# A decoder layer on one core: query rows sent as diagonal blocks, self attention over pairs of batches, preparation and second layer norm drawn into the self loop, one product for the maxima

## The reference, cut to what matters

```python
# x: 16 batches x 56 tokens x 128; ctx: 16 x 1500 x 128; bias: 16 x 1500; 16 heads of 8
x = x + self_attention(layernorm(x))                  # qkv with bias, scores / sqrt(8), softmax, projection
x = x + cross_attention(layernorm(x), ctx, bias)      # bias added to the scores before the softmax
x = x + experts(layernorm(x))                         # top 4 of 32 experts, and one shared expert
```

## Time and profile before

| what | value |
|---|---|
| median of 3 runs | 533.33 us (532.56 to 533.93) |
| the profiled execution, its own time | 532.37 us |
| its span in the trace | 530.6 us |
| PE busy, share of the span | 455.5 us, 86% |
| DVE | 377.0 us, 71% |
| ACT | 345.5 us, 65% |
| POOL | 261.1 us, 49% |
| mean granted clock of PE | 0.93 of full speed |

### The profile page before, as it was taken

One profiled execution on the slowest core, in us unless ns is written; L12 is line 12 of the kernel. 1 busy time (PEld: TensorE's weight loads), 2 busy tenths in 40 slices (PEclk: granted clock), 3 DMA queues, 4 the chain that ended last, 5 costly groups with the idle time before them and its releaser, 6 DMA issues.

```text
span 530.6 us, 16284 instructions
## 1 busy us (share of the span) xinstructions
PE 455.5 (86%) x6841; PEld 297.1 (56%) x6841; DVE 377.0 (71%) x603; ACT 345.5 (65%) x716; POOL 261.1 (49%) x207
## 2 busy tenths in 40 slices
PE   3225898568999999999999999999989886799995
PEld 2013676234677677667677667667766653344442
DVE  6752445878777777777777777777778234899994
ACT  6802654424788788788788888888876772355552
POOL 4399005458668568558657756751400310145430
PEclk9757889865999999999999999999999997899998
DMA  6991069183768674794694695483202020011101
GB/s 129 226 260 56 3 129 209 53 236 110 128 205 204 124 165 143 123 194 124 114 208 125 125 186 107 115 94 97 89 12 61 13 51 1 16 45 46 30 1 35
DMA packets 79758, 58.24 MB, mean 110 GB/s; under 512 B 62350, under 2 KB 69830, under 8 KB 79686
## 3 DMA queue, kind: packets, MB, share of 16 engines
q1 hardware_dynamic: 78886, 57.15, 48.3%
q0 software_dynamic: 512, 0.03, 0.1%
q10 hardware_dynamic: 288, 0.03, 0.0%
HBM read 17.01 MB, written 0.46 MB: 33 GB/s over the span
## 4 chain that ended last, share of the span: by engine, by line
PE 61%; DVE 12%; issue 10%; ACT 5%; POOL 2%; DVEq 0%; POOLq 0%; ACTq 0%
PE ps L925 18%; PE ps L814 12%; PE ps L903 6%; DVE mx L1514 3%; PE ps L817 3%; DVE v L1609 3%; ACT v L1269 3%; PE ps L368 3%; PE ps L370 3%; PE ps L369 3%; PE ps L824 2%; PE ps L744 2%; PE ps L747 2%; PE ps L745 2%; PE ps L962 1%
## 5 line engine op out<-in xcount | busy, mean ns | idle before, releaser
L1514 DVE TENSOR_REDUCE mx<-ps 120x2 f32<-120x1000 f32 x192 | 221.1, 1195 | 66.8 <-PE ps L903 66.7
L1209 ACT ACTIVATE p<-ps 125x448 f32<-125x448 f32 x288 | 140.6, 543 | 9.0 <-PE ps L925 7.5
L925 PE MATMUL ps<-qall,ks 128*125 128x224 f16 x768 | 134.4, 278 | 6.0 <-ACT p L1209 2.8
L925 PEld LDWEIGHTS ps<-qall,ks 128*125 128x125 f16 x768 | 75.7, 137 | 46.4 <-ACT p L1209 23.1
L620 POOL TENSOR_TENSOR k<-k,zero 128x500 f16<-128x500 f32 x45 | 45.9, 1021 | 92.8 <-ACT k L1145 92.8
L814 PE MATMUL ps<-p,v 125*27 125x168 f32 x1280 | 72.8, 312 | 0.0
L600 POOL TENSOR_TENSOR ch<-ctx,zero 128x1536 f16<-128x1536 f32 x16 | 44.0, 2748 | 41.5 <-issue 27.8
L624 POOL TENSOR_TENSOR k<-k 128x500 f16<-128x500 f32 x45 | 51.1, 1135 | 3.5
L610 POOL TENSOR_TENSOR ch<-ctx,ch 128x1536 f16<-128x1536 f32 x16 | 51.4, 3212 | 1.3
L1209 ACT ACTIVATE wnat<-ps 125x448 f32<-125x448 f32 x96 | 47.0, 541 | 7.5 <-PE ps L925 7.5
L903 PE MATMUL ps<-ks,qall 31*56 31x500 f16 x768 | 44.8, 407 | 6.7 <-DVE mx L1514 6.6
(11 more groups left out here) (178 smaller groups left out, 811.6 us busy)
## 6 DMA issues: line engine op xcount, KB each, us to landing
ks<-k SPq DMA_DIRECT2D x48, 375.0 KB
ctx<-in_ctx SPq DMA_DIRECT2D x16, 672.0 KB
ks<-in_L_ffn_W SPq DMA_DIRECT2D x48, 64.0 KB, 2.0
qall<-late SPq DMA_DIRECT2D x6, 448.0 KB, 6.9
ks<-brow SPq DMA_DIRECT2D x32, 46.9 KB
qall<-qd SPq DMA_DIRECT2D x3, 448.0 KB, 8.5
ctx<-in_ctx SPq DMA_DIRECT2D x16, 78.0 KB
qall<-qconst SPq DMA_DIRECT2D x1, 896.0 KB, 10.3
```

Source lines behind the costliest of these rows:

```text
L925: last = mm(stb[half][0:KP, 224 * (g % 2):224 * (g % 2) + 224], ks[c % 3][:, g, KP * s:KP * s + KP], qall[:, g, 3 * r + c].rearrange("p h ...
L1209: A(p[s % 4][0:KP, 448 * half:448 * half + 448], stb[half][0:KP, 0:448], ACT.Exp, scale=SCALE).then_inc(exp_done, 1)
L1514: V.tensor_reduce(mx[:, h:h + 2, k // 2], mxb[0:120, 2 * pair:2 * pair + 2, 0:CH], axis=AX.X, op=ALU.max).then_inc(mx_read, 1)
```

## The change

`qall` changes its order from group, batch, head to group, head, batch. POOL fills it with zeros once, and the queries of 32 partitions go straight from `q1` and `q2` into the rows of their own head: four transfers a row for all batches of self attention, and the same for cross attention, now in the parts of two and of fourteen batches. The mask, `qd`, `first_queries` and `second_queries` go. Self attention runs over pairs of batches, the second at partitions 64 to 119 (11 steps instead of 19). Batch 0 and the keys of batch 1 are prepared inside these steps. LN2 is split into one tile and six. The maxima of the cross loop take one product of 16 columns. The two selects of `pairsel` move on POOL behind the last key split. The diff, cut to its core (what stands behind a # names the engine or the place):

```diff
-PARTS = [((0, B // 2), (B // 2, B)), ((0, 4), (4, B // 2), (B // 2, B))]
-EARLY = 1
-OUT_STEP = 13
+PAIRS = B // 2
+PARTS = ((0, 2), (2, B))
+PREP = {1: (0, "K0"), 2: (0, "K1"), 3: (0, "K2"), 4: (0, "V0"), 5: (0, "V1"), 6: (0, "V2"),
+        7: (1, "K0"), 8: (1, "K1"), 9: (1, "K2")}
+OUT_STEP, TURN_STEP, Q_STEP = 5, 7, 8
...
-        qall = sb("qall", [128, G, B, HG, S], F16)
+        qall = sb("qall", [128, G, HG, B, S], F16)
+        LN_TILES = (TILES, ((0, 1), (1, TT)), TILES)
+        QX = ((0, S * PARTS[0][1]), (S * PARTS[0][1], T))
+        def query_rows(engine, n, k, row, part, done):
+            a, z = ((0, B),)[k] if n == 0 else PARTS[k]
+            src = (q1, q2)[part]
+            for j in range(HG):
+                engine.dma_start(qall[32 * j + row:32 * j + 32:4, :, j, a:z].rearrange("p g b q -> p g (b q)"),
+                                 src[32 * j:32 * j + 32, S * a:S * z]).then_inc(done, 16)
...
             load_ctx(0)
+            sp.wait_ge(qconst_ok, 1)
+            sp.wait_ge(qzero_ok, 2)
+            for j in range(HG):
+                sp.dma_start(qall[32 * j + HI_ROW:32 * j + LO_ROW + 1:4, :, j].rearrange("p g b q -> p g (b q)"),
+                             qconst[0:2].rearrange("p (o x) -> p o x", o=1).to_broadcast([2, G, T])).then_inc(qfill_ok, 16)
+            sp.wait_ge(q1_ok, 2)
+            for row in range(2):
+                query_rows(sp, 0, 0, row, 0, qs_ok[0])
             load_ctx(1)
...
             bias_rows(0)
             bias_rows(1)
-            key_stacks(0)
             transpose_ctx(1)
             load_ctx(3)
+            key_stacks(0)
+            sp.wait_ge(st_done, 1)
+            sp.wait_ge(q1_ok, 3)
+            for row in range(2):
+                query_rows(sp, 1, 0, row, 0, qx_ok[0][0])
             transpose_ctx(2)
             load_ctx(4)
             key_stacks(1)
+            sp.wait_ge(st_done, PAIRS)
+            sp.wait_ge(q1_ok, 4)
+            for row in range(2):
+                query_rows(sp, 1, 1, row, 0, qx_ok[1][0])
+            sp.wait_ge(q2_ok, 4)
+            query_rows(sp, 1, 1, 2, 1, qx_ok[1][1])
             transpose_ctx(3)
             load_ctx(5)
...
+            def zero_queries(n):                                     # POOL
+                memset(qall[:, 2 * n:2 * n + 2].rearrange("p g h b q -> p (g h b q)").bitcast(F32), 0.0
+                       ).then_inc(qzero_ok, 1)
...
+            zero_queries(0)
             rstd_of(0, 0)
             rstd_of(0, 1)
+            zero_queries(1)
...
+            rstd_of(1, 0)
             split_first(2)
             split_second(2)
-            rstd_of(1, 0)
-            rstd_of(1, 1)
             for j in range(3):
                 split_keys(1, j)
+            rstd_of(1, 1)
             split_first(3)
             split_second(3)
...
+            def self_max_rows(half):                                 # PE
+                pe.wait_ge(mself_ok, 4 * half + 4)
+                for upper in range(2):
+                    rows = slice(64 * upper, 64 * upper + S)
+                    for b in range(8):
+                        last = mm(ps[0:8, (4, 2)[half] + upper, S * b:S * b + S],
+                                  mself[rows, half, :, :, b].rearrange("p g j -> p (g j)"),
+                                  ident[rows, rows], start=True, stop=True)
+                last.then_inc(mselft_psum, 1)
...
+            def self_step(s):                                        # PE
+                k = s % 2
+                if s < PAIRS:
+                    pe.wait_ge(mself_row[s // 4], 2 * 16)
...
+                    for g in range(G):
+                        for u in range(2):
+                            b = 2 * s + u
+                            last = mm(sbank[64 * u:64 * u + S, g // 2, 224 * (g % 2):224 * (g % 2) + 224],
+                                      kself[:, g, S * b:S * b + S], qall[:, g, :, b], start=True, stop=True)
+                    last.then_inc(st_done, 1)
+                    if s == 0:
+                        self_max_rows(1)
...
+                if 0 <= s - 3 < PAIRS:
+                    tr(pair_misc[:, 0:128], tok[:], ident[:]).then_inc(misc_done, 1)
+                if s in PREP:
+                    b, use = PREP[s]
+                    prepare[use[0]](0, b, int(use[1]))
+                if 0 <= s - 1 < PAIRS:
+                    pair_times_v(1 - k)          # 16 products, the two batches at rows 0 and 64, banks 6 and 7
+                if 0 <= s - 2 < PAIRS:
+                    pick_pair()
...
                 elif use == "mt":
                     pe.wait_ge(mcol_ok, 3 * r + c + 2)
-                    for j in range(HG):
-                        last = mm(misc[0:G, S * j:S * j + S], mcol[:, j::HG], fold[:], start=True, stop=True)
-                    last.then_inc(misc_done, 1)
+                    mm(misc[0:H, 0:S], mcol[:], fold[:], start=True, stop=True).then_inc(misc_done, 1)
...
                         last = mm(stb[half][0:KP, 224 * (g % 2):224 * (g % 2) + 224],
                                   ks[c % 3][:, g, KP * s:KP * s + KP],
-                                  qall[:, g, 3 * r + c].rearrange("p h q -> p (h q)"),
-                                  start=True, stop=True)
+                                  qall[:, g, :, 3 * r + c], start=True, stop=True)
...
+            query_rows(act, 0, 0, 2, 1, qs_ok[1])                    # ACT, before the self loop
+            for row, part in ((0, 0), (1, 1), (2, 0)):
+                act.dma_start(ks[2][row::4, :, 0:T], k12[:, part, 0:T]).then_inc(kself_in, 16)
...
+                elif j == 0:
+                    act.wait_ge(brow_ok, 1)                          # ACT, key part K0 of batch 0
+                A(k32[:, cols], use_bank(r, c, f"K{j}")[:, 0:CH], ACT.Copy).then_inc(use_read(r, c, f"K{j}")[0], 1)
...
+                if s == Q_STEP:                                      # ACT
+                    A(q1[:, a:z], chain_bank[:, 0:z - a], ACT.Copy).then_inc(q1_ok, 1)
+                    act.wait_ge(q2_ok, 3)
+                    query_rows(act, 1, 0, 2, 1, qx_ok[0][1])
...
             add_to_x(LN_TILES[1][1], flat_bank(0, 768), x_ok)        # DVE
             norm_stats(1, 1)
-            norm_apply(1, 1)
...
+            take_round(0, -2, 2, 0)
+            norm_apply(1, 1)
+            for k in range(1, ROUNDS // 2):
                 take_round(0, -2, 2, k)
```

More of the change, by code:

```diff
@@ L117, in part_of, with prep_index, self_uses, self_index @@
 def part_of(b):
-    return [a <= b < z for a, z in PARTS[1]].index(True)
-def early(r, c):
-    return isinstance(r, int) and 3 * r + c < EARLY
+    return [a <= b < z for a, z in PARTS].index(True)
+def prep_index(b, use):
+    return PREP_ORDER.index((b, use)) if (b, use) in PREP_ORDER else None
 def round_of(d):
     return (1, d + 3) if d < 3 else (2, d - 3)
[L132 to L147, removed]
+def self_uses(s):
+    return [u for u, lag in (("tr", 3), ("sel", 2)) if 0 <= s - lag < PAIRS]
+def self_index(s, use):
+    return sum(len(self_uses(k)) for k in range(s)) + self_uses(s).index(use)
 def build(nc, x_d, ctx_d, bias_d, qkv_w, qkv_b, proj_w, proj_b, wq, wk, wv, wo,
@@ L298, in build @@
         mselfr_ok = sem("mselfr_ok")
-        mself_row = sem("mself_row")
+        mself_row = [sem(f"mself_row{n}") for n in range(2)]
         st_done = sem("st_done")
@@ L687, in split_experts @@
                                         ).then_inc(wh_ok, 1)
+            for n, row0 in enumerate((0, 32)):
+                pool.wait_ge(pairsel_step, n + 1)
+                select(out=pairsel[:], in_=pairsel[:], compare_op=ALU.not_equal, fill=1.0, base=-row0,
+                       pattern=[[-2, NP], [-1, 2], [0, HE]], channel_multiplier=1).then_inc(pairsel_step, 1)
             rstd_of(2, 0)
@@ L712, in transpose_norm @@
             def transpose_norm(n, half, bank, done):
[L714 to L717 removed]
+                a, z = LN_TILES[n][half]
+                pe.wait_ge(xn_ok, TT * n + z)
+                out = flat_bank(bank, 128 * (z - a)) if z - a > 4 else ps[:, bank]
+                for j in range(a, z):
+                    last = tr(out[:, 128 * (j - a):128 * (j - a) + 128], xn[:, j], ident[:])
                 last.then_inc(done, 1)
@@ L772, in _ @@
                 project(SELF_W, half, 4 + half, q_psum)
+            for half in range(2):
                 project(SELF_W + 1, half, 6 + half, k_psum)
@@ L877, in router_logits @@
+            pe.wait_ge(pick_ok, 1)
+            for s in range(PAIRS + 3):
+                self_step(s)
             def router_logits(half, bank):
@@ L1203, in exponential @@
+            self_max_rows(0)
+            for s in range(PAIRS + 3):
+                self_step(s)
+            norm_out(1, 1, 0, xt_psum, 3)
+            act.wait_ge(pv_done, PAIRS)
             def exponential(r, c, s, half):
-                tile = B + KT * (3 * r + c) + s
+                tile = PAIRS + KT * (3 * r + c) + s
```

(7 more changed lines are left out.)

577 lines of the change are left out of this document (253 added, 324 removed).

## The result

The changed kernel takes 517.91 us, the median of 4 runs (517.17 to 518.73), where the kernel before took 532.98 beside it (532.56 to 533.93). The ratio is 0.9715, with a 95% interval of 0.9693 to 0.9737: 15.1 us faster. The prediction was 508.2 with a range of 499 to 519, and a gain of 25. The direction and the range held; ten of the 25 us did not come.

What follows compares the result with a forecast made beforehand. PE bounds the cross loop; before it, waits and single steps do. First cross scores 19.6 us earlier, plus 1.0 for masks and 4.5 for products, give 25.1: from 533.33 to 508.2 us, range 499 to 519.

Steps and rivals of the forecast that it cites:

- Loop period: Cross loop, bound by PE: three of four products mt go, 0.28 us in each of 15 iterations, 4.5 us with the copy.
- strided queries: Cross loop: score products reading four runs of 56 elements cost zero extra; the opposing slower case had chance 0.04.
- single maximum product: Cross loop: one product mt in place of four saves 3 x 0.09 = 0.28 us per iteration.
- first cross scores: Milestone before the cross loop: from 128.83 to 109.2, about 17.6 us after the query projection.
- removed masks: Cross loop: the last masks, 2.33 us of ACT in the chain, go; partly covered, worth 1.0 us.
- Selects: Before self attention: PE's 4.46 us wait for pairsel goes; moving the selects on POOL costs nothing.
- First maximum round: First milestone, in self attention: from 30.68 to 27.5, bounds 25 and 31, summed from projections, copies, issues and landing.
- First self scores: Second milestone: from 52.84 to 41.0, with 3.4 us for the block of 16 small products.
- Self loop: Third milestone, the loop's end: from 95.89 to 74.5, at 3.0 us per step of a pair of batches.
- bias operation: Self step 0: 2.81 us on DVE delays ACT's first key part; step 3 starts near 50.3 instead of 48.5.
- Behind the loop: Loop's end to cross query projection: 17.1 us, reaching 91.6 instead of 111.47; six normalization tiles cost 4.
- The first one: Pairs do not run side by side, or the path behind the loop grows: 517.5 with steps alone, 523 with all; chance 0.20.

Runs made afterwards that it cites:

- second profile of the changed kernel: The changed kernel, unedited, run once more beside its variants as the base for small differences: 518.75 us.
- that run: The kernel before with only the two pairsel selects moved late on POOL, PE's wait put ahead of the experts: 527.95 us against 534.77.
- the kernel of four products: The changed kernel with the four products mt per batch, their copy and transfer put back in the cross loop: 520.66 us.

## Why the prediction was right, and where ten microseconds went

- **Loop period, strided queries, single maximum product: right.** 5.5 us were predicted behind the first cross scores, 5.7 came, and 4.6 in the second profile of the changed kernel (517.3 - 120.11 = 397.2); the score products cost what they did; the single product gives 4.4 us by the periods. The 1.0 us for the removed masks wasn't tested, and the clock differs in that stretch.
- **Selects: right.** "I see no use of theirs before the experts: nothing" holds, and the wait they caused was worth 4 to 4.5 us by the profile of that run.
- **First maximum round: wrong by 4.8 us.** Two steps failed. "POOL's new zero fill [...] hidden behind the projections" priced only POOL's own time; it held LN1 on DVE for 3.8 us, and the run without that gave 2.9 back at the end. "SP's context loads [...] are passed by four fills and eight query issues" priced only when the context is wanted. What it missed is that the load of batch 1 moves beside the keys: the landing, taken as 5 us, was 6.9 to 7.2 with it and 2.8 without. I had measured the old crowd and removed it without asking which transfer comes in its place. In the terms of the sum: the projections ended at 32.30 - 12.40 = 19.9 and not at 16.4, and the landing took 1.9 more. The seven issues on ACT took 5.8 us and not 4.2, but they ran beside the key copies, so that the last one ended 5.4 us behind the projections where 5.8 were costed.
- **First self scores: 2.2 us better.** The block was costed at 3.4 us and took 2.75, and the four other rounds with the copy and the hand-over took 43.58 - 39.65 = 3.9 us (the end of the block is at 39.7) where 5.3 were costed.
- **Self loop: short by 3.7 us.** Part of it is a slip of the sum. From step 1 at 45.5 to step 3 at 48.5 the prediction leaves 3.0 us, its price of one step, where two lie between. Measured, step 0 takes 3.9 us (4.5 costed), steps 1 and 2 take 53.85 - 47.48 = 6.4 (4.8 with the bias operation), the next five 16.1 (15.0), and the rest up to the output projection 10.8 (9.2). The bias operation was overpriced, 1.8 us in the sum and 0.56 us of ACT's time in the trace, and that hid a part of the slip. Most steps take 3.1 to 3.2 us, not 3.0, and the one with the first output projection 3.5. The heads product takes 0.92 us instead of the 0.45 costed: its stationary operand is 112 columns wide now, where it was 56, and PE's weight loads for it are busy for 0.86 us of that, where they were for 0.49 of 0.55 before. The "four query issues on ACT (2.4 us)" were in the sum, but as 2.4 us ahead of ACT's copies in a drain of 9.2; they took 2.9, and moved by one step they give 2.1.
- **Behind the loop: short by 3.5 us.** Here the mechanism was in the sum. "Six tiles cost 1.7 to 6.4; I take 4" was a mean between two rows. The prediction itself says that the changed POOL starts the splits "just here", so both of them were to be expected on the six tiles, and the upper bound was the likely value: 6.28. The output projection of six tiles, at half clock, took 2.93 us where 1.6 was costed.
- **The sums.** Besides the missing step, 27.5 and 13.3 make 40.8 and not 41.0, the terms behind the loop add up to 17.4 and not 17.1, and those of the first cross scores to 17.8 and not 17.6. Added up rightly, the prediction's own terms give about 511.5 us. So some 3 of the 10 missing us are addition, and not mechanism. The 0.6 us by which the first cross scores fell short wasn't followed further.
- **Rivals.** The first one had two causes, and only the second came true. The pairs do run side by side: the eight products L833 of a pair take 0.51 us, where four of one batch took 0.42, and a step takes 3.2, not 4.85. The path behind the loop did grow, by 3.5 us beyond the sum, and transfers came late. That the time lies at the 517.5 that this rival gave for slow steps alone is chance, and so is it in part that the range held.

The rule behind two of the misses, LN1 and LN2, is in the Trainium skill (SBUF — State Buffer, Who interferes with whom): VectorE in a two-port mode, which `tensor_scalar` can enter, shares a pair of ports with GpSimd; whichever issues first has the pair for its whole instruction, and the other fully blocks. The rows agree, to 0.1 us: 90.94 against 90.86, 94.10 against 94.03; no row shows the mode. The same page of the Trainium skill (SBUF: two separate sides) also says that an operation with two SBUF inputs is only blocked by a GpSimd operation that reads SBUF. The bias operation fits that: held by the split until 38.60, and then running 2.66 us beside a fill that had started at 38.54.

## What to carry to other kernels

Price every new or moved instruction of GpSimd by what VectorE does in the same microseconds, fills too: lay the two timelines side by side, and let a VectorE operation from SBUF to SBUF that would start inside an instruction of GpSimd, and all that is queued behind it, wait until that instruction ends. A wait of one line, that puts GpSimd's work behind the short VectorE work, cost nothing here, where GpSimd had slack. When transfers are removed from a crowded stretch, ask which load the queue's order now brings into it, and hold back by a wait the loads that nobody needs yet.

## What the runs showed of the hardware that was not expected

- The DVE operations that POOL held were from SBUF to SBUF. The two lines below (line by line, least, median and greatest ns) set the normalization beside the reductions from PSUM: POOL is busy for 52% of the span, and not one of 192 reductions was held.

```profile
L1339 DVE TENSOR_SCALAR xn<-xs,mv,rstd x21: 334/342/3242, 7.5 to 430.9; 128x128 f32<-128x128 f32 x21
```

```profile
L1516 DVE TENSOR_REDUCE mx<-ps x192: 1181/1192/1202, 86.6 to 397.9; 120x2 f32<-120x1000 f32 x192
```

- A block of 16 small float32 products takes 3.8 times as long as in float16 (2.75 and 0.73 us, both at half clock), though the trace shows only two records for each float32 product.
- The time from first to second maximum copy differed by 1.3 us between two profiles of the same kernel (18.79 and 20.08) and by 2.5 with the kernel of four products (17.57), with the granted clock between 0.50 and 0.67 at 115 to 120 us and between 0.62 and 1.00 in the next 5 us. That is as much as some edits here are worth; a period within one clock level tells more than a total.
